# A four-layer graph network in one kernel: normalisation, output and scaling moved to ScalarE, a sum moved to VectorE, new instruction orders

## The reference, cut to what matters

```
def _layernorm(x, axis=-1, eps=1e-05):
    m = mean(x); v = var(x)
    return (x - m) / sqrt(v + eps)

L0: q, k, v = heads of x @ W_qkv (8 heads of 64)
    attn = softmax(q k^T / 8, masked) * 0.33 + 0.33 * adj + 0.33 * exp(-adj)
    out = (attn @ v) @ W_out + b_out
L1: H = (adj != 0); w = first row of adj
    Dn = 1 / (H @ w), 0 where that is 0;   Be = 1 / column sums of H, 0 where that is 0
    conv(x, W, b) = Dn * (H @ (Be * (H^T @ (x @ W^T)))) + b
    h = layer_norm(relu(conv(x, W1, b1))) * gamma + beta
    out = conv(h, W2, b2) + x
L2: Xw = X @ Wv + bv; sj, si = its dot products with the halves of aw
    e = leaky_relu(sj + si + ab, 0.2)
    T = adj * exp(e) / (row sum + 1e-12)
    out = relu(sum over k = 0, 1, 2 of T^k X @ Wk[k] + bk[k])
L3: agg = (adj @ x) / max(row sum of adj, 1e-6)
    out = relu(concat(x, agg) @ W^T)

x = _layernorm(x + L0(x)); x = _layernorm(x + L1(x)); x = _layernorm(x + L2(x)); x = _layernorm(x + L3(x))
```

## Time and profile before

| what | value |
|---|---|
| median of three runs | 1407.92 us |
| the profiled execution's own time | 1405.77 us |
| its span, first to last instruction | 1404.0 us |
| mean granted clock of TensorE | 0.986 |
| PE busy | 1309.8 us (93%) |
| DVE busy | 1165.8 us (83%) |
| ACT busy | 896.5 us (64%) |
| POOL busy | 623.8 us (44%) |
| DMA | 28.32 MB, 20 GB/s |

### The profile page before, as it was taken

The page is one execution under the profiler, slowest core; times in us unless marked ns, Lnnn a source line. Parts: engine busy times, 40 slices in busy tenths (PEclk is TensorE's granted clock), DMA queues, the critical chain, the costliest instruction groups (busy, mean ns, idle before and its releaser), DMA issues.

```text
span 1404.0 us, 32421 instructions
## 1 busy us (share of the span) xinstructions
PE 1309.8 (93%) x9705; PEld 1124.8 (80%) x9705; DVE 1165.8 (83%) x3449; ACT 896.5 (64%) x2677; POOL 623.8 (44%) x1094
## 2 busy tenths in 40 slices
PE   4799999999999999999999999999999999999975
PEld 3688888888888888888888888888888888888863
DVE  2588888888888888888888888888888888888884
ACT  3467666667666666666666766666666666676641
POOL 3135444344544344545434454434544543445442
PEclk9899999999999999999999999999999999999996
DMA  5000000000000000000000000000000000000000
GB/s 184 14 14 21 20 7 20 12 20 20 20 8 19 12 20 20 20 20 7 20 12 20 20 20 8 19 12 20 20 20 20 7 20 12 20 20 20 9 8 8
DMA packets 35588, 28.32 MB, mean 20 GB/s; under 512 B 7664, under 2 KB 34416, under 8 KB 35568
## 3 DMA queue, kind: packets, MB, share of 16 engines
q1 hardware_dynamic: 33984, 27.27, 6.2%
q0 software_dynamic: 176, 0.52, 0.2%
q10 hardware_dynamic: 1408, 0.27, 0.1%
HBM read 19.67 MB, written 8.39 MB: 20 GB/s over the span
## 4 chain that ended last, share of the span: by engine, by line
issue 35%; POOL 24%; DVE 21%; PE 12%; ACT 3%; POOLq 1%; DVEq 1%; ACTq 0%
POOL rs L1435 9%; DVE prob L1118 8%; POOL rs L1433 4%; PE PS L520 3%; POOL resid L1472 3%; POOL resid L1474 3%; DVE neg_max L1109 3%; POOL xout L1490 2%; ACT yT_hi L908 2%; PE PS L396 2%; POOL gate L1458 2%; PE PS L397 2%; POOL yT_lo L1503 1%; DVE xT_lo L1051 1%; PE PS L400 1%
## 5 line engine op out<-in xcount | busy, mean ns | idle before, releaser
L1433 POOL TENSOR_TENSOR rs<-mv,eps_c 128x1 f32<-128x1 f32 (+1 forms) x288 | 60.3, 209 | 339.5 <-DVE mv L1059 339.5
L1118 DVE SCALAR_TENSOR_TENSOR prob<-prob,rl,gate 128x128 f32<-128x128 f32 x512 | 200.2, 451 | 6.6 <-DVE rl L1115 0.4
L827 ACT ACTIVATE prob<-PS,neg_max 128x128 f32<-128x128 f32 x512 | 179.9, 385 | 2.4 <-DVE neg_max L1109 2.4
L1435 POOL TENSOR_TENSOR rs<-rs,mhalf 128x1 f32<-128x1 f32 (+1 forms) x288 | 166.1, 577 | 22.5
L810 ACT ACTIVATE qk<-PS 128x512 f32<-128x512 f32 x128 | 76.6, 599 | 120.4 <-PE PS L474 120.4
L470 PE MATMUL PS<-xT_hi,wqk_hi 128*128 128x256 f32 x512 | 137.5, 290 | 6.8 <-DVE wk_lo L1044 4.6
L1499 POOL TENSOR_TENSOR z<-z,bk_bc 128x256 f32<-128x256 f32 x64 | 48.4, 775 | 203.0 <-ACT z L886 203.0
L471 PE MATMUL PS<-xT_hi,wqk_lo 128*128 128x256 f32 x512 | 133.7, 283 | 0.0
L827 ACT ACTIVATION_READ_ACCUMULATOR prob<-PS,neg_max 128x1 f32 x512 | 115.3, 225 | 0.0
L470 PEld LDWEIGHTS PS<-xT_hi,wqk_hi 128*128 128x128 f32 x512 | 98.1, 192 | 14.3 <-issue 11.9
L474 PE MATMUL PS<-xT_lo,wqk_hi 128*128 128x256 f32 x512 | 103.1, 283 | 0.0
(11 more groups left out here) (215 smaller groups left out, 4370.0 us busy)
## 6 DMA issues: line engine op xcount, KB each, us to landing
xin<-in_x_dram SPq DMA_DIRECT2D x32, 256.0 KB, 2.8
out_dram<-xout SPq DMA_DIRECT2D x32, 256.0 KB, 2.2
adj_in<-in_adj_dram SPq DMA_DIRECT2D x32, 128.0 KB, 2.1
wqkv_raw<-in_L_gnn_W_qkv_dram SPq DMA_DIRECT2D x1, 1536.0 KB, 7.5
w_raw<-in_L_gnn_W_dram SPq DMA_DIRECT2D x3, 512.0 KB, 12.1
mask_bc<-in_nodemask_dram SPq DMA_DIRECT2D x32, 32.0 KB, 2.8
wk_raw<-in_L_gnn_Wk_dram SPq DMA_DIRECT2D x3, 256.0 KB, 10.5
wout_raw<-in_L_gnn_W_out_dram SPq DMA_DIRECT2D x1, 512.0 KB, 12.8
```

The lines of the kernel that those rows point to most:

```text
L827: last = act.activation(prob[:, t, h, :], PS[:, bank, k * P:(k + 1) * P], ACT.Exp, bias=neg_max[:, t, h:h + 1], accum_out=row_sum[:, t, h: ...
L1118: last = dve.scalar_tensor_tensor(prob[:, t, h, :], prob[:, t, h, :], rl[:, t, h:h + 1], gate[:, t], ALU.mult, ALU.add)
L1433: step.done(pool.tensor_tensor(rs[:, n, gs, 0], mv[:, n, gs, 1], eps_c[:].to_broadcast([P, graphs]), ALU.add))
L1435: return pool.tensor_tensor(rs[:, n, gs, 1], rs[:, n, gs, 0], mhalf[:].to_broadcast([P, graphs]), ALU.pow)
```

## The change

Each point says what is done; the diff below is cut to its core.

1. The four layer norms' last step goes from DVE (x1, x2, x3) and POOL (the output) to ACT, as one activation with a scale and a shift from `rs`. POOL therefore computes both: after the scale's two operations a third writes -mean * scale.
2. x1 is written once, doubled (`x1t`). W1 is halved when it is split, and POOL's residual add is one instead of two.
3. The scaling of H^T by Be goes from POOL to ACT (`BHT_`), later in the order.
4. The sum over hyperedge weights is made on DVE from `adj_in` and the first adjacency row `wrow`, which a new DMA spreads over the partitions; `D_` on PE, `wone`, the copy `dcol` and `rA` go.
5. The bias behind W2 is added by DVE where it empties the product (`hw_`), with the scale; ACT's `hw_` and `u_` go.
6. The layer-2 vectors come from four columns of Z2 (two scaled by 0.2 in set-up), so `Z_` on DVE is one operation, and Z2 has 260 columns for 258.
7. Waits are finer: `S_` and `PT_` wait by halves, `xT2_` and `AT_` by graph, DVE's waits for its own results are put further behind.
8. SP's loads wait for their own readers and are issued in three parts, `adj_in` with `wrow` first, then `xin`, then the mask.
9. The orders on PE, ACT, DVE and POOL and the table of banks are new.

```diff
+            def reload(i):
+                sp.wait_ge(dve_Dsum, i * G)
+                sp.wait_ge(pe_adjT, i)
+                sp.wait_ge(dve_deg, i)
+                sp.wait_ge(act_gate, i)
+                sp.wait_ge(pool_gate, i)
+                sp.sem_inc(sp_past, 1)
+                sp.dma_start(adj_in[:], ag[:, bass.ds(i * G, G), :]).then_inc(a_in, 16)
+                sp.dma_start(wrow[:], adj[bass.ds(i * G, G), 0:1, :].rearrange("g a m -> (a g) m").partition_broadcast(P))\
+                    .then_inc(w_in, 16)
+                sp.wait_ge(pe_xT0, i)
+                sp.wait_ge(pool_resid0, i)
+                sp.sem_inc(sp_past, 1)
+                sp.dma_start(xin[:], xg[:, bass.ds(i * G, G), :]).then_inc(x_in, 16)
+                sp.wait_ge(act_mbc, i * G)
+                sp.wait_ge(act_mrow, i * 2)
...
-            def D_(i):
-                pe.wait_ge(dve_HT, i + 1)
-                pe.wait_ge(dve_wone, i + 1)
-                for g in range(G):
-                    last = pe.matmul(PS[:, bank_D, 2 * g:2 * g + 2], HT[:, g, :], wone[:, g, :], start=True, stop=True)
-                last.then_inc(pe_D, 1)
...
             def PT_(i, t):
-                pe.wait_ge(dve_attn, 2 * (i * G + t + 1))
                 for h in range(HEADS):
+                    if h % (HEADS // 2) == 0:
+                        pe.wait_ge(dve_attn, 2 * (i * G + t) + 1 + h // (HEADS // 2))
...
+            def normalise(dst, src, n, g, scale_ready, value, done):       # on ACT
+                act.wait_ge(scale_ready, value)
+                act.activation(dst, src, ACT.Identity, scale=rs[:, n, g, 1:2], bias=rs[:, n, g, 0:1]).then_inc(done, 1)
+            def BHT_(i):
+                act.wait_ge(dve_Be, i + 1)
+                for g in range(G):
+                    act.activation(BHT[:, g], HT[:, g], copy, scale=Be[:, g:g + 1]).then_inc(act_BHT, 1)
...
+                def Dsum_(g):                                              # on DVE
+                    dve.scalar_tensor_tensor(dprod[:, g], adj_in[:, g], 0.0, wrow[:, g], ALU.not_equal, ALU.mult,
+                                             accum_out=dcol[:, g:g + 1]).then_inc(dve_Dsum, 1)
+                def hw_(g):
+                    dve.scalar_tensor_tensor(hw[:, g], PS[:, bank_hw[g], 0:D], rs[:, NORMH, g, 1:2], bw_bc[:], ALU.mult, ALU.add)\
+                        .then_inc(dve_hw, 1)
...
+            def scale_shift(step, n, g, ready, value, factor=1.0):         # on POOL
+                step.done(scale(step, n, g, ready, value, factor))
+                settle(pool)
+                return pool.tensor_scalar(rs[:, n, g, 0:1], mv[:, n, g, 0:1], rs[:, n, g, 1:2], -1.0, ALU.mult, ALU.mult)
```

More of the change, by code:

```diff
@@ L603, in Z_ @@
                 for c in range(DC):
[L604 removed]
+                    last = low(PS[:, bank_Z2[g], 0:D + 4], both(xT2, A, c, g), both(wk2, A, c), c == DC - 1)
                 last.then_inc(pe_Z2, 1)
@@ L1088, in counts, with deg_, Be0_, Be_ @@
+                def deg_():
+                    dve.wait_ge(a_in, i * 16 + 16)
+                    dve.wait_ge(dve_degm, i)
+                    dve.tensor_reduce(degf[:], adj_in[:], AX_X, ALU.add).then_inc(dve_deg, 1)
+                def Be0_():
+                    step.wait(counted['cnt'])
+                    counted['Be'] = step.count(dve.tensor_scalar(cnt[:], cnt[:], 1.0, None, ALU.max))
+                def Be_():
+                    step.wait(counted['Be'])
                     dve.reciprocal(Be[:], cnt[:]).then_inc(dve_Be, 1)
+                def Dsum_(g):
@@ L1106, in max_ @@
+                def Dn_():
+                    step.wait(counted['r'])
+                    dve.scalar_tensor_tensor(Dn[:], dcol[:], 0.0, drec[:], ALU.is_gt, ALU.mult).then_inc(dve_Dn, 1)
                 def max_(t):
@@ L1136, in mv0_ @@
                     aggregate(step, counted[t], NORM0, t, dve_mv0)
-                def x1_(t):
-                    normalise(x1[:, t], ys0[:, t], NORM0, t, pool_rs0, i * G + t + 1, dve_x1)
-                return step, xT0_, incidence, counts, dcol_, Dn_, max_, norm_, OT_, y0_, bn0_, mv0_, x1_
+                return (step, xT0_, incidence, cnt_, deg_, Be0_, Be_, Dsum_, Dn0_, Dn1_, Dn_, max_, rl_, norm_, OT_, y0_, bn0_,
+                        mv0_)
             def back(j):
@@ L1267, in group @@
                 if F:
-                    fstep, _, incidence, counts, dcol_, Dn_, max_, norm_, fOT_, y0_, bn0_, mv0_, x1_ = front(i)
+                    (fstep, _, incidence, cnt_, deg_, Be0_, Be_, Dsum_, Dn0_, Dn1_, Dn_, max_, rl_, norm_, fOT_, y0_, bn0_,
+                     mv0_) = front(i)
                 if B:
-                    (bstep, ax_, hb_, hstats_, hT_, y1_, x2_, xT2_, xT3_, Z_, z2_, gmax_, al_, all_, den_, Y_, Yl_, o2_, y2_, bn2_, mv2_, x3_, deg_, zb_,
-                     o3_) = back(j)
+                    (bstep, ax_, hb_, bnh_, mvh_, hT_, hw_, y1_, bn1_, mv1_, xT2_, xT3_, Z_, z2_, gmax_, al_, all_, den_, rden_, Y_, Yl_, o2_, y2_,
+                     bn2_, mv2_, degb0_, degb_, zb_, o3_, y3_, bn3_, mv3_) = back(j)
+                if B:
+                    degb0_()
                 if F:
@@ L1283, in group @@
                 if B:
-                    deg_()
-                if F:
-                    counts()
-                if B:
-                    y1_(0)
-                    y1_(1)
-                    x2_(0)
-                    x2_(1)
+                    mvh_(0)
+                    hT_(0)
+                    bnh_(1)
+                    hT_(1)
+                    mvh_(1)
+                    hw_(0)
                 if F:
                     max_(1)
+                if B:
+                    hw_(1)
+                    y1_(0)
+                if F:
+                    rl_(0, 1)
+                if B:
+                    bn1_(0)
+                    mv1_(0)
+                    y1_(1)
+                    bn1_(1)
+                    degb_()
+                    mv1_(1)
+                if F:
+                    rl_(0, 0)
+                    Dsum_(0)
+                    rl_(1, 0)
                     norm_(0, 0)
+                    norm_(0, 1)
+                    Dsum_(1)
                 if B:
```

588 lines of the change are left out of this document (294 added, 294 removed).

## The result

The changed kernel takes 1605.85 us (median of four runs, 1604.54 to 1606.9) beside 1408.06 us of the kernel before: ratio 1.1404 [1.1385, 1.1424], 198 us slower. The direction and the place were forecast; the size was not: the forecast was 1452 us, in a range of 1395 to 1474.

What follows compares the result with a forecast made beforehand. It took in-order PE, busy 93%, and its waits as the bound. Per pass -0.68 -2.1 +0.15 +0.3 +0.7 +1.0 +2.1 = +1.5; thirty groups +45, shaded to 42, total +44: 1450, by the median 1452 us, range 1395 to 1474.

Steps and rivals of the forecast that it cites:

- the load, which decides: At PE's `xT0_`: `xin`, issued late behind `degf`, `adj_in` and `wrow`, makes PE wait 2.1 us a pass.
- Rival C: On TensorE: four waits a pass let the granted clock fall, +0.4 us a pass, 1465 us; chance 0.05.
- `D_`, -0.68: On PE: the `D_` matmuls go, saving 0.68 us a period.
- The old waits, -2.1: PE's existing waits at `PT_`, `y1_`, `Z_` and `xT3_`, 2.1 us a pass, all given back before new ones are added.
- `y1_(1)` 0.5 for +0.3: PE waits 0.3 us at `y1_(1)`, because `max_(1)` stands between `hw_(0)` and `hw_(1)` on DVE.
- `xT2_` 1.1 for +0.7: PE waits 0.7 us at `xT2_` for y1 and mv on DVE, then POOL, then ACT.
- `PT_` 0.7 for +1.0: PE waits 1.0 us at the second half of `PT_(i, 0)` for DVE's norms, slowed by POOL's `ys` add.
- `hT_(0)` nothing for +0.15: PE waits 0.1 to 0.2 us at `hT_(0)`, since ACT ends a group with `out_` and frees late.
- The chain from `mv1_(1)` to `xT2_`: POOL's scale plus shift takes 1.3 us after `mv`, then 0.4 of ACT; each normalisation comes 0.5 us later.
- the add's price: POOL's `ys` add beside DVE's norms lengthens them by some 0.9 us, bounds 0 and 1.3.
- Rival A: The load is hidden after all, leaving sooner or wanted later: period 40.8, 1388 us; chance 0.13.
- Rival B: The load is late but the early waits don't come: 1402 us, or 1408 with load wait 2.3; chance 0.10.

Runs made afterwards that it cites:

- experiment 2: Changed kernel with only the `wrow` load moved from ahead of `xin` to behind the mask: 1451.45 us, 1.0319 to the kernel before.
- experiment 5: Kernel before, with the `wrow` DMA added between `adj_in` and `xin` plus one DVE wait, nothing reading it: 1407.74 us, 1.0009.
- experiment 4: Changed kernel with 34 unread identity transposes on PE ahead of `xT0_`, inside the load wait: 1530.06 us, 1.0878 to the kernel before.
- experiment 6: Kernel before, with only the row sum `degf` on DVE moved from `counts` to behind `Z_(1)`: 1510.4 us, 1.0737.
- experiment 1: Changed kernel with SP's `xin` and mask block moved ahead of the `adj_in` and `wrow` block: 1404.38 us, 0.9981 to the kernel before.
- experiment 3: Changed kernel with only `deg_()` on DVE moved ahead of the first `Dsum_`, load order kept: 1422.94 us, 1.0117 to the kernel before.

## Why the prediction was wrong in size

**The step that failed is "the load, which decides".** Its mechanism was right and its price was not: it was to cost a wait of 2.1 us a pass at a full clock; it cost 4.1 and a half clock worth 2.5. The term mis-sized in it is the landing of `xin`, and the clock was left out of the sum. The chain from the start of `si_(1)` on PE (821.07):

| link | forecast | measured |
|---|---|---|
| to the end of `degf` | 0.35 | 0.24 |
| release to issue | 0.48 | 0.30 |
| `adj_in` and `wrow` issued ahead | 1.14 | 1.14 |
| landing of `xin` | 2.8 ("up to 0.5 more") | 5.0 |
| PE wants `xin` | 2.5 (its terms add to 2.4) | 2.6 |
| wait | 2.3, taken as 2.1 | 4.08 |

Four links are within 0.2 us, and with a landing of 2.8 the wait would be 1.9. The landing behind `wrow` was the one number without a row. The prediction bounded it by 0.5 because its rows of 512 B looked like those of `adj_in`; `adj_in` lands in 2.1 us and `wrow` in 5.0, and `xin`, queued behind it, lands late too (experiments 2 and 5). With no row for it, the bound should have been wider. The estimate by the Trainium skill (SBUF — State Buffer, "The DMA setup-cost knee"), 2.6 us, was further off still.

**Rival C had the right mechanism and the wrong price.** It had a chance of 0.05 and +0.4 us a pass. Its argument against, "1.00 with waits of 0.8", said nothing of a wait of 2 us. The trace of the kernel before had one, in its set-up: 2.21 us ahead of the first `xT0_`, and half the clock from 0.8 us behind it on.

```profile
19.52 0.63 PE L459 MATMUL PS<-ident,xin 128*128 128x128 f32 x4 [2.21 <-DVE w3t_lo L1044]
```

```profile
20.28:23.69 3.41, 2.86 (x13) 2.86 (x14) 0.69 (x1) 0.50 (x1) 0.00 (x0) 0.50 0.83 298
```

PE had been busy for only 5.06 of the first 19.5 us, so this proves nothing for the loop, but it was a reason to give C more weight. Measured: +2.5 a pass (experiment 4). It follows from the first error only in part: at 2.7 us of wait the clock fell too (experiment 6), at 1.4 it did not (experiment 2). The forecast's 2.1 lay between, and no run here tells what it does there.

**The sum with measured terms.** Experiment 1 gives all but the load: 41.19 - 41.47 = -0.28 a pass, where the forecast's terms without the load add to -0.63. Then -0.28 + 4.1 + 2.5 = 6.3, and 47.79 - 41.47 = 6.32. The -0.28 itself is 0.85 less busy (40.15 to 39.30) and 0.57 more idle (41.47 - 40.15 = 1.32, 41.19 - 39.30 = 1.89). The thirty periods from group 1's `xT0_` on are 188 of the 200 us of span. Another 10 are lost ahead of them, from group 0's `xT0_` to group 1's, where the forecast had 2. That stretch in the kernel before, the changed one and experiment 1:

```profile
19.52:57.39 37.87, 24.60 (x152) 20.81 (x152) 17.38 (x49) 17.69 (x58) 11.26 (x11) 0.82 0.16 53
19.44:67.72 48.28, 30.02 (x151) 24.59 (x152) 16.57 (x49) 18.75 (x59) 10.17 (x9) 0.66 0.13 44
19.90:65.49 45.59, 29.15 (x151) 23.74 (x152) 16.56 (x49) 18.61 (x59) 10.15 (x9) 0.70 0.14 44
```

Experiment 1 loses 7.7 of them too, at a clock of 0.70, though no load is late there; what in the new order does it, no run separates.

**Its other steps.**
- `D_`, -0.68: near the 0.85 less of busy time, though no run takes it alone. The old waits, -2.1, were read off distances between starts, and so must the new ones be: the idle time in brackets is smaller, because a matmul counts as busy to its end. The 0.51 before `PT_`'s second half is 0.7 by starts (four transposes take 816.59 - 816.18 = 0.41, and the four before them took 1.12), and the 0.98 before `xT2_`'s second half is 1.1 (814.79 - 813.42 = 1.37, less 0.27 for a pair).
- By starts, then: `y1_(1)` 0.5 for +0.3 (0.23 idle, for DVE's `hw`; it starts 0.82 behind `y1_(0)`, and a pair takes 0.35), `xT2_` 1.1 for +0.7, `PT_` 0.7 for +1.0, `hT_(0)` nothing for +0.15, and some 0.4 at `S_` that the forecast did not have (0.18 idle, for ACT's `qk`). That is 2.7 for 2.15, and with -0.68 and -2.1 it gives -0.1, beside -0.28 measured: the new waits were taken too small, and nothing shows that the old ones were taken too large.
- That experiment 2 comes to 1451.45, beside a forecast of 1452, is luck in part: its load wait was 0.7 smaller and its other terms 0.35 larger a pass, and its first stretch was 7.8 us longer (45.70 for 37.87) where 2 were forecast.
- The chain from `mv1_(1)` to `xT2_` is right in kind. Scale plus shift, forecast at 1.3, was 1.3 for the first graph and 1.5 for the second, which PE waits for. The normalisation on ACT, priced at 0.42 by `x_twice`, is 0.61 in the mean (the line at the end of this list). `x_twice` scaled by a constant; this one reads scale and shift from memory. The Trainium skill (ScalarE: Activation LUTs, "What ACT_TABLE_LOAD costs") gives 93 ns for each such operand, and the trace agrees: 0.42 + 0.19 = 0.61.
- At `PT_` the add's price was right (0.9; 1.0 measured), but PE came later to the second half, since `xT2_` ahead of it had waited longer.
- The sum with `accum_out`, taken as 0.3: 0.30, with 0.08 for reading the accumulator.
- Rival A (the load hidden: 1388) is what experiment 1 makes true by hand, at 1404: of the 16 us between, some 11 are the 0.37 a pass by which the terms above were off, the rest is in the first group. Rival B (no early waits) fell: `xT2_` and `PT_` waited 33 times each, 1.0 and 0.6 us idle in the mean.

```profile
L851 ACT ACTIVATE x<-ysb,rs 128x256 f32<-128x256 f32 x128 | 78.5, 614 | 87.3 <-POOL rs L1524 87.3
```

**Left open.** Why `wrow` is slow to land: it is one row of 512 B per graph, read by all 128 partitions, and whether the repeated source or something else holds it, no run separates. Why the clock falls in seven passes of experiment 3. Why the first group is 8 us longer in experiments 1 and 2. The early `ys` add in the kernel before was not tried, so 0.9835 is not split between the change and that order.

## What to carry to other kernels

When an edit moves the instruction that releases a buffer, follow the release to the DMA queue, list all that is issued there ahead of the load that PE wants next, and put that load first if its own waits allow it. Where the landing time of a transfer behind a new neighbour has no row, measure it or leave its bound wide. A wait of some us in each pass of a loop bound by TensorE may cost twice, as idle time and as the slow matmuls behind it; here it did at 2.7 and 4.1 us and not at 1.4, so price both cases.

## What the runs showed that was not expected

- A broadcast of two rows of 512 B to 128 partitions (128 KB written) lands in 4.5 to 5.0 us, where 128 KB of distinct rows land in 2.1, and it holds up the 256 KB transfer behind it in the same queue from 2.8 to 5.0 us.
- Useless matmuls in a wait made the kernel 76 us faster (1605.85 to 1530.06), all of it clock.
- A wait of 1.4 us a pass left the granted clock at 1.00; 2.7 us, in another order, brought it to half for 3.4 us in most passes and 6.8 in four, 4.15 us for 6.8 us in each. With no wait at the load and two of 0.99 and 0.78 us behind each other it was at half for 3.4 us in seven passes of some thirty (experiment 3).
